# A two-layer decoder on one core: last cross-attention and feed-forward of four sequences as one unrolled block, and a new key order in the first self-attention

## The chip, the cores and the metric

The kernel runs on one core of a Trainium2 chip. Its engines are TensorE (PE, matmuls; PEld is its weight load), VectorE (DVE), ScalarE (ACT), GpSimd (POOL) and SyncE (SP, which here issues every DMA). Matmuls read SBUF and write PSUM. The metric is the device time of one execution in microseconds (us), lower is better.

## The reference, cut to what matters

The input x has 4 sequences of 1024 tokens and 256 features. Two decoder layers follow, each of self-attention, cross-attention to a context of 154 keys, and a feed-forward, each with a residual and a layer norm behind it. The change touches the first of these six parts and the last two.

```python
x = _layernorm(x + _L0_attn_ref(...))    # 16 heads of 16 features, causal bias
...
# last cross-attention: 16 heads of 16 features, padded keys masked
attn = jnp.einsum('bhqd,bhkd->bhqk', Q, K) * scale
attn = jax.nn.softmax(jnp.where(mask, -jnp.inf, attn), axis=-1)
x = _layernorm(x + out @ Wo + bo)
# last feed-forward
xr = mu_r * x + (1 - mu_r) * x_prev
xk = mu_k * x + (1 - mu_k) * x_prev
r = jax.nn.sigmoid(xr @ W_r.T)
k_act = jnp.square(jax.nn.relu(xk @ W_k.T))
x = _layernorm(x + r * (k_act @ W_v.T))
```

## The kernel before

The program has four stages, one behind the other, with a barrier of all engines between them. Stage one is the first self-attention, stage two the first cross-attention, stage three the first feed-forward with the second self-attention, and stage four the second cross-attention with the last feed-forward. Stages one to three take all four sequences in one unrolled block; stage four is a loop over the sequences (`nc.Fori(0, B)`, L1911), with a barrier at the end of each turn and semaphores that are cleared.

**Attention in two passes.** Stages one and four find the row maxima first: a first pass of scores (`first_scores` L375, `first_scores1` L2069) goes into PSUM tile psA, VectorE takes the negated maximum (L674, L2367), and the maxima are transposed, split into three bf16 parts and carried through DRAM into extra rows of the query stack (`max_dram`, `max1_dram`). A second pass (L389, L2077) has keys on the partitions and goes into psB; ScalarE takes the exponential from there into `pbuf` or `pb1` (L507, L2193), and the products with the values (`values` L400, `values1` L2091) add up in psO. Queries and keys are held as stacked bf16 parts, which also travel through DRAM. A column of ones beside the values gives the denominators; these go through DRAM to a tile of reciprocals (`reciprocals`), by which GpSimd scales the outputs (`scale_values`). psA and psB have two buffers each.

**Stage one.** The work is 128 steps, one for each of 16 head groups (4 heads of one sequence) and 8 tiles of 128 tokens. Step k issues the first pass for query tile 7 - k % 8 of group k // 8, and, 10 steps behind (LEAD), the second pass for key tile (k - 10) % 8. The mask is causal, so query tile j has j + 1 blocks of 128 keys, and key tile i has 8 - i blocks of queries. A step first issues all scores of both passes in turn, then the value products of the key tile of the step before, then a projection for another sequence if one is due (`qk_unit`, `v_unit`, `out_unit`).

**Stage four.** One turn of the loop loads the sequence, projects the keys and values of its context, transposes x, projects the queries, splits them into parts (ACT L2179 and L2182, POOL L2262, DVE L2292 and L2293), stores and loads the stack, runs the two passes over the 4 head groups with the second pass 2 groups behind (LEAD1), projects the output (L2023 and L2033), normalises, transposes, mixes each token with the one before it (ACT L2205, DVE L2390), and runs the three feed-forward products (`gemm`, L2000), with Relu and Square for the keys (L2210, L2213), Sigmoid for the gate (L2217) and the gated product on VectorE (L2396, L2399). SP stores the output tile by tile.

## Time and profile before

| what | value |
|---|---|
| three runs, median | 2812.36 us (2809.44 to 2812.92) |
| profiled execution | 2812.02 us |
| its span, first to last instruction | 2810.2 us |
| mean granted TensorE clock | 0.891 of full |
| TensorE busy in the span | 2175.3 us, 77% |
| VectorE, ScalarE, GpSimd busy | 1471.6, 1200.9, 612.2 us |

Instructions outside the span take 1.8 us of the profiled execution. In the trace, stage one lies from 0 to 914 us, stage two to 1505, stage three to 2109.8, and stage four to the end; its four turns begin near 2117, 2290, 2464 and 2637 us. A group of instructions is named by line, engine, operation and tiles; the arrow stands between what is written and what is read. All matmuls of `gemm` have one line, so those are told apart by their tiles. "Busy" of an engine is the union of its instructions' times.

### The profile page before, as it was taken

To read this page: it belongs to the slowest core of one execution; us is meant where nothing else is said; L and a number is where in the kernel's file an instruction comes from. 1 tells how busy PE (TensorE), PEld (TensorE's weight loads), DVE (VectorE), ACT (ScalarE), POOL (GpSimd) and SP (SyncE) were. 2 spreads that over 40 slices of the span, in tenths; PEclk is the share of its full clock that TensorE was granted. 3 is DMA by queue.
4 is the path that set the end of the run, shared out by engine and by line. 5 is a ranking of instruction groups with operands and counts; after the bars stand their busy time and mean duration, and the time that the engine had idled before them with its cause. 6 is when DMAs were issued, how large, how long until landed. Compare 5 with 4: busy or idle time off the path is not lost. (4 is left out here: it accounts for less than half of the span.)

```text
span 2810.2 us, 32610 instructions
## 1 busy us (share of the span) xinstructions
PE 2175.3 (77%) x11571; PEld 1209.3 (43%) x11586; DVE 1471.6 (52%) x2718; ACT 1200.9 (43%) x2635; POOL 612.2 (22%) x725
## 2 busy tenths in 40 slices
PE   4688888888887899999995348889994856747566
PEld 2233343343343555656553225556662332423324
DVE  3554465465662466666673676583543334443444
ACT  1245435435443565555552637574221332314232
POOL 4611210310011100000002665462311110211102
PEclk7899999999998899999997569999996886868768
DMA  7424324324221100000002001000007124161341
GB/s 159 112 49 90 68 59 88 70 59 70 46 65 33 50 5 18 16 18 16 8 9 68 15 0 36 6 25 12 25 17 124 36 58 64 32 103 35 69 61 31
DMA packets 129404, 135.42 MB, mean 48 GB/s; under 512 B 35405, under 2 KB 110033, under 8 KB 129170
## 3 DMA queue, kind: packets, MB, share of 16 engines
q1 hardware_dynamic: 129266, 133.62, 21.6%
q8 instruction: 82, 1.34, 0.2%
q14 instruction: 56, 0.46, 0.1%
HBM read 95.10 MB, written 38.47 MB: 48 GB/s over the span
## 5 line engine op out<-in xcount | busy, mean ns | idle before, releaser
L507 ACT ACTIVATE pbuf_sb<-psB 128x512 f32<-128x512 f32 (+1 forms) x608 | 326.7, 573 | 348.7 <-PE psB L397 342.8
L674 DVE TENSOR_REDUCE negm_sb<-psA 128x1 f32<-128x1024 f32 (+6 forms) x352 | 340.1, 1019 | 151.0 <-PE psA L385 149.7
L394 PE MATMUL psB<-qst_sb,kst_sb 99*128 99x512 bf16 (+3 forms) x768 | 234.0, 338 | 58.3 <-ACT pbuf_sb L507 47.6
L1030 ACT ACTIVATE pw_sb<-psA,nmx_sb 128x154 f32<-128x154 f32 x512 | 192.0, 387 | 194.5 <-DVE nmx_sb L1121 194.5
L383 PE MATMUL psA<-kst_sb,qst_sb 96*128 96x512 bf16 (+3 forms) x768 | 197.8, 334 | 59.9 <-DVE negm_sb L674 52.8
L1121 DVE TENSOR_REDUCE nmx_sb<-psA 128x4 f32<-128x616 f32 x128 | 102.2, 799 | 176.8 <-PE psA L898 176.8
L2193 ACT ACTIVATE pb_sb<-psB 128x512 f32<-128x512 f32 x160 | 89.0, 596 | 170.3 <-PE psB L2082 168.4
L2073 PE MATMUL psA<-kst_sb,qst_sb 97*128 97x160 bf16 x512 | 86.1, 323 | 95.8 <-issue 66.6
L411 PE MATMUL psO<-pbuf_sb,V_sb 128*32 128x512 f32 (+3 forms) x1536 | 153.6, 503 | 0.2 <-ACT pbuf_sb L507 0.2
L394 PEld LDWEIGHTS psB<-qst_sb,kst_sb 99*128 99x128 bf16 x768 | 75.1, 98 | 168.3 <-ACT pbuf_sb L507 145.5
L2367 DVE TENSOR_REDUCE negm_sb<-psA 128x4 f32<-128x640 f32 x128 | 100.0, 821 | 81.2 <-PE psA L2073 76.8
L383 PEld LDWEIGHTS psA<-kst_sb,qst_sb 96*128 96x128 bf16 x768 | 58.1, 98 | 166.2 <-DVE negm_sb L674 106.5
L1358 PE MATMUL psO<-va_sb,pat_sb 128*128 128x256 f32 x512 | 118.2, 384 | 9.8 <-DVE pat_sb L1743 9.8
L851 PE MATMUL psO<-XT_sb,wq_x_sb 128*128 128x512 f32 x256 | 122.2, 601 | 0.0
L1070 POOL TENSOR_SCALAR std_sb<-mv_sb 128x1 f32<-128x1 f32 x32 | 7.3, 228 | 503.4 <-DVE mv_sb L1148 503.4
L851 PE MATMUL psO<-wo_x_sb,ox_sb 128*128 128x256 f32 x512 | 115.4, 379 | 0.8 <-ACT ox_sb L1013 0.8
L1358 PE MATMUL psA<-qa_sb,ka_sb 128*128 128x512 f32 x256 | 115.1, 592 | 0.0
L1358 PEld LDWEIGHTS psO<-va_sb,pat_sb 128*128 128x128 f32 x512 | 97.6, 192 | 33.6 <-DVE pat_sb L1743 13.7
L2073 PEld LDWEIGHTS psA<-kst_sb,qst_sb 97*128 97x128 bf16 x512 | 52.2, 129 | 136.6 <-issue 77.3
L385 PE MATMUL psA<-masku_sb,identb_sb 128*128 128x128 bf16 x512 | 107.0, 223 | 0.0
L1716 DVE TENSOR_REDUCE nma_sb<-psA 128x1 f32<-128x1024 f32 x32 | 39.1, 1222 | 129.2 <-PE psA L1358 129.2
L1030 ACT ACTIVATION_READ_ACCUMULATOR pw_sb<-psA,nmx_sb 128x1 f32 x512 | 103.9, 203 | 0.0
(264 smaller groups left out, 4463.0 us busy)
## 6 DMA issues: line engine op xcount, KB each, us to landing
rden_sb<-dens_dram SPq DMA_DIRECT2D x128, 128.0 KB, 2.7
parts_dram<-parts_sb SPq DMA_DIRECT2D x32, 384.0 KB, 2.4
qst_sb<-parts_dram SPq DMA_DIRECT2D x96, 128.0 KB, 4.4
kst_sb<-parts_dram SPq DMA_DIRECT2D x96, 128.0 KB, 7.0
qst_sb<-parts_dram SPq DMA_DIRECT2D x48, 256.0 KB, 9.1
x_dram<-X_sb SPq DMA_DIRECT2D x64, 128.0 KB, 1.7
parts_dram<-partsb_sb SPq DMA_DIRECT2D x16, 384.0 KB, 6.9
xT_sb<-xT SPq DMA_DIRECT2D x4, 1024.0 KB, 5.1
```

Of the source, the lines that this page charges most:

```text
L383: nc.tensor.matmul(psA[:, k, at + lo:at + hi], qst[0:QK_ROWS, gg % 3, h, j * P:(j + 1) * P], kst[0:QK_ROWS, gg % 3, h, lo:hi], start=True, ...
L385: last = nc.tensor.matmul(psA[:, k, at + w - P:at + w], identb[:, :], masku[:, :], start=False, stop=True)
L394: last = nc.tensor.matmul(psB[:, k, at:at + hi - lo], kst[0:MAX_ROWS, gg % 3, h, i * P:(i + 1) * P], qst[0:MAX_ROWS, gg % 3, h, lo:hi], st ...
L411: last = nc.tensor.matmul(psO[32 * h:32 * h + 32, c, lo - c * 512:hi - c * 512], V[:, b % 2, i, at:at + 32], pbuf[:, i % 2, h, lo:hi], sta ...
L507: nc.scalar.activation(pbuf[:, i % 2, heads[0]:heads[-1] + 1, lo:hi], psB[:, (nb.n - 1) % 2, 0:len(heads) * (hi - lo)] .rearrange("p (h n) ...
L674: nc.vector.tensor_reduce(out=negm[:, gg % 2, heads[0]:heads[-1] + 1, j], in_=psA[:, (na.n - 1) % 2, :].rearrange("p (h n) -> p h n", h=le ...
L851: last = nc.tensor.matmul(dst, lhsT(i), rhs(i), start=(i == 0), stop=(i == n - 1))
L1030: last = nc.scalar.activation(pw[:, m % 2, h, :], psA[:, m % 2, at:at + K], ACT.Exp, bias=nmx[:, m % 2, h:h + 1], accum_out=psx[:, m % 3, ...
L1121: nc.vector.tensor_reduce(out=nmx[:, m % 2, :].rearrange("p (b a) -> p a b", a=2), in_=psA[:, m % 2, :].rearrange("p (a n) -> p a n", a=2) ...
L1358: last = nc.tensor.matmul(dst, lhsT(i), rhs(i), start=(i == 0), stop=(i == n - 1))
L2073: last = nc.tensor.matmul(psA[:, k, at:at + KP], qst1[0:R1, 4 * g + h, j * P:(j + 1) * P], kst1[0:R1, 4 * g + h, :], start=True, stop=True)
L2367: nc.vector.tensor_reduce(out=negm1[:, g, :, j].rearrange("p (a b) -> p a b", a=2), in_=psA[:, (na.n - 1) % 2, :].rearrange("p (a n) -> p ...
```

## The change

**Stage one.** A table KEY_ORDER gives both the key tile of the second pass and the query tile of the first pass in a step, so that every step has nine score blocks for each head. `values` is cut into the two halves of the query tokens (c = 0 and c = 1), and these are issued behind the second and behind the first unit of scores of a step.

**Stage four.** The loop is gone. One block of 24 units takes all sequences: unit gg issues the first pass of head group gg and the second pass of group gg - 2; a unit has 8 steps j. In each step, `side_tasks(gg, j)` names what else is due there: for the next sequence the transposes ("xp"), query gemms ("q"), and keys and values of the context ("kp", "vp"); for the sequence just finished its output projection ("o"); for the one before it the transposes ("xf"), the key products ("kg") and the gate and value products ("rv"). The first pass has one PSUM buffer of 1024 columns, psA[:, 0]; the side tasks share the two halves of psA[:, 1]. The query split is wholly on GpSimd, and so is the addition of the output bias. Tiles are doubled for two sequences in flight (XE, v1, v1r, kst1), the query stack has four slots and OT1 six. The barriers and clears of the loop are gone; one clear of semaphores is added behind stage one.

```diff
+    KEY_ORDER = (3, 2, 1, 0, 7, 6, 5, 4)
+    def query_tile(k):
+        return KEY_ORDER[(k - LEAD) % 8]
...
-                first = first_units(7 - k % 8) if k < UNITS else []
-                second = second_units(s % 8) if 0 <= s < UNITS else []
+                first = first_units(query_tile(k)) if k < UNITS else []
+                second = second_units(KEY_ORDER[s % 8]) if 0 <= s < UNITS else []
                 for u in range(max(len(first), len(second))):
...
+                    if u == 0 and s >= 1:
+                        values((s - 1) // 8, KEY_ORDER[(s - 1) % 8], exps_at[s - 1], 1)
+                    if u == 1 and s >= 1:
+                        values((s - 1) // 8, KEY_ORDER[(s - 1) % 8], exps_at[s - 1], 0)
...
-                if 1 <= s:
-                    values((s - 1) // 8, (s - 1) % 8, exps_at[s - 1])
...
+    nc.sync.sem_clear(range(a_full.num, x_stored.num + 1))
...
-    with top, nc.Fori(0, B) as b:
...
+        q, u = gg // 4, gg % 4
+        e, o, p = q - 2, q - 1, q + 1
+        if 0 <= e < B:
+            if u == 0 and j in (1, 3):
+                out += [("xf", e, j - 1), ("xf", e, j)]
+            if u == 0 and j in (6, 7):
+                out += [("kg", e, j - 6, 0)]
+            if u == 1 and j in (0, 1):
+                out += [("kg", e, j, 1)]
+            if u in (1, 2) and 3 <= j < 7:
+                out += [("rv", e, 4 * (u - 1) + j - 3)]
+        if 0 <= o < B and u == 3:
+            out += [("o", o, j)]
+        if p < B:
+            if u == 0 and j in (0, 2):
+                out += [("xp", p, j), ("xp", p, j + 1)]
+            if u == 0 and j in (4, 5):
+                out += [("q", p, 0, j - 4)]
+            if u == 1 and j == 2:
+                out += [("q", p, 1, 0)]
+            if u == 2 and j < 3:
+                out += [(("q", p, 1, 1), ("kp", p), ("vp", p))[j]]
...
+                for j in range(NT):
+                    if gg < GROUPS:
+                        first_scores(gg, j)
+                    if 0 <= gs < GROUPS:
+                        second_scores(gs, j // 4, j % 4)
+                        if j % 4 == 3:
+                            second_scores(gs, j // 4, 4)
+                    if j == 1 and 1 <= gs <= GROUPS:
+                        values(2 * gs - 1)
+                    if j == 5 and 0 <= gs < GROUPS:
+                        values(2 * gs)
+                    for key in side_tasks(gg, j):
...
```

On the other engines of stage four, ScalarE takes in step j its exponentials, then the copy-out in steps 2 and 6, then its part of the side task. VectorE takes the residual or gated product of the side task of step j - 1, then the maxima of step j, then the normalisation for step j - 2; the mixing is in steps 5 and 6 of a unit with u = 0, the reciprocals of group gg - 3 in step 5. GpSimd scales group gg - 3 in step 7 and adds the bias in step 5 where u = 2. SP issues in each unit the stack of the next group, then the denominators' journey of group gg - 3, then stores of parts and outputs, and the maxima last.

How the order moves, in three places.

TensorE, stage one, the end of a step with query tile 2 and key tile 3 and the value products of key tile 2, before (L383 is the first pass, L394 the second, L385 the mask, L411 the value products):

```order
L383 MATMUL psA<-kst_sb,qst_sb 128x384
L385 MATMUL psA<-masku_sb,identb_sb 128x128
L383 MATMUL psA<-kst_sb,qst_sb 128x384
L385 MATMUL psA<-masku_sb,identb_sb 128x128
L394 MATMUL psB<-qst_sb,kst_sb 128x512 x4
L411 MATMUL psO<-pbuf_sb,V_sb 32x256 x4
L411 MATMUL psO<-pbuf_sb,V_sb 32x512 x4
```

And in the change, the middle and end of the step with query tile 2 and key tile 2 (L380, L391, L382 with L394 as masks, and L408 for the value products of key tile 3; L349 is a projection):

```order
L408 MATMUL psO<-pbuf_sb,V_sb 32x512 x4
L380 MATMUL psA<-kst_sb,qst_sb 128x384
L382 MATMUL psA<-masku_sb,identb_sb 128x128
L380 MATMUL psA<-kst_sb,qst_sb 128x384
L382 MATMUL psA<-masku_sb,identb_sb 128x128
L391 MATMUL psB<-qst_sb,kst_sb 128x256
L394 MATMUL psB<-maskl_sb,identb_sb 128x128
L391 MATMUL psB<-qst_sb,kst_sb 128x256
L394 MATMUL psB<-maskl_sb,identb_sb 128x128
L408 MATMUL psO<-pbuf_sb,V_sb 32x128 x4
L391 MATMUL psB<-qst_sb,kst_sb 128x512 x4
L349 MATMUL psA<-wqkv_sb,xT_sb 128x256 x2
```

The value products stood behind all scores of a step; now one half stands behind the first unit of scores and the other behind the second, and four second-pass units follow them.

ScalarE, stage four, before (end of the feed-forward of a turn; L2217 is the Sigmoid):

```order
L2210 ACTIVATE dk_sb<-psB 128x512
L2213 ACTIVATE kact_sb<-dk_sb 128x512
L2210 ACTIVATE dk_sb<-psB 128x512
L2213 ACTIVATE kact_sb<-dk_sb 128x512
L2217 ACT_TABLE_LOAD
L2217 ACTIVATE rg_sb<-psA 128x256 x8
```

And in the change, from unit 9 on (L2338 is the Sigmoid, L2308 the exponential, L2284 and L2289 the queries):

```order
L2308 ACTIVATE pb_sb<-psB 128x512 x2
L2338 ACT_TABLE_LOAD
L2338 ACTIVATE rg_sb<-psA 128x256
L2308 ACT_TABLE_LOAD
L2308 ACTIVATE pb_sb<-psB 128x512
L2338 ACT_TABLE_LOAD
L2338 ACTIVATE rg_sb<-psA 128x256
L2308 ACT_TABLE_LOAD
L2308 ACTIVATE pb_sb<-psB 128x512
```

One load of a function table stood ahead of eight Sigmoids; now one stands ahead of each Sigmoid and one ahead of the exponential behind it. From here to the end of the block ScalarE has 41 such loads, where the loop had two in each of its four turns.

TensorE, stage four, before (feed-forward):

```order
L2012 MATMUL psB<-ident_sb,X_sb 128x128 x12
L2000 MATMUL psB<-xk_sb,wk_f_sb 128x512 x8
L2000 MATMUL psA<-wr_f_sb,xr_sb 128x256 x2
L2000 MATMUL psA<-wv_f_sb,kact_sb 128x256 x2
L2000 MATMUL psA<-wr_f_sb,xr_sb 128x256 x2
L2000 MATMUL psA<-wv_f_sb,kact_sb 128x256 x2
```

And in the change, in unit 9 (L2153 first pass, L2163 second pass, L2178 and L2182 value products, L2105 `gemm`):

```order
L2105 MATMUL psA<-wr_f_sb,xr_sb 128x256 x2
L2105 MATMUL psA<-wv_f_sb,kact_sb 128x256 x2
L2153 MATMUL psA<-kst_sb,qst_sb 128x160 x4
L2163 MATMUL psB<-qst_sb,kst_sb 128x512
L2105 MATMUL psA<-wr_f_sb,xr_sb 128x256 x2
L2105 MATMUL psA<-wv_f_sb,kact_sb 128x256 x2
L2153 MATMUL psA<-kst_sb,qst_sb 128x160 x4
L2163 MATMUL psB<-qst_sb,kst_sb 128x512
L2178 MATMUL psO<-pb_sb,v1r_sb 128x512
L2182 MATMUL psO<-pb_sb,v_sb 32x512 x4
L2105 MATMUL psA<-wr_f_sb,xr_sb 128x256 x2
L2105 MATMUL psA<-wv_f_sb,kact_sb 128x256 x2
```

The gate and value products of one sequence, two instructions each, stand now between the score passes of another.

## Rows read from the trace of the kernel before

**Rows 1.** Page, parts 1 and 2: busy shares; tenths in 40 slices of 70 us
```profile
PE 2175.3 (77%) x11571; PEld 1209.3 (43%) x11586; DVE 1471.6 (52%) x2718; ACT 1200.9 (43%) x2635; POOL 612.2 (22%) x725
...
PE   4688888888887899999995348889994856747566
...
PEclk7899999999998899999997569999996886868768
```

**Rows 2.** Busy time of each engine in stretches (from:to, length, then the columns)
```profile
core 0: us, PE busy (x) PEld busy (x) DVE busy (x) ACT busy (x) POOL busy (x), PEclk, DMA share, GB/s
124.00:844.00 720.00, 614.48 (x4125) 276.22 (x4125) 386.59 (x537) 342.04 (x630) 109.98 (x122) 0.98 0.32 66
2109.80:2157.80 48.00, 14.42 (x48) 8.99 (x48) 11.14 (x23) 9.29 (x15) 8.75 (x17) 0.68 0.72 139
2637.00:2810.20 173.20, 110.71 (x484) 60.21 (x484) 71.62 (x152) 51.14 (x88) 26.74 (x48) 0.77 0.31 59
2637.00:2693.80 56.80, 25.65 (x112) 15.49 (x112) 23.60 (x39) 8.68 (x15) 7.22 (x13) 0.65 0.73 118
2693.80:2740.00 46.20, 37.76 (x192) 13.20 (x192) 17.37 (x34) 24.34 (x45) 2.35 (x1) 0.80 0.12 29
2740.00:2757.00 17.00, 15.04 (x73) 10.04 (x73) 1.93 (x3) 2.19 (x4) 4.70 (x2) 1.00 0.23 67
2770.00:2810.20 40.20, 24.25 (x80) 16.17 (x80) 18.61 (x44) 14.13 (x22) 6.23 (x16) 0.80 0.08 26
```

**Rows 3.** Chain that ended last, in the last sequence: start us, us, what
```profile
2680.45 13.32 DMA qst_sb<-parts_dram
...
2777.90 10.18 PE psB L2000 x16
```

**Rows 4.** Stage one, 124 to 844 us: PE groups by shape; then one wait
```profile
L394 PE MATMUL psB<-qst_sb,kst_sb 99*128 99x512 bf16 x358 | 136.9, 394 | 45.2 <-ACT pbuf_sb L507 37.6
L383 PE MATMUL psA<-kst_sb,qst_sb 96*128 96x512 bf16 x346 | 121.1, 385 | 37.8 <-DVE negm_sb L674 32.0 <-DVE X_sb L628 2.2
...
ACT pbuf_sb L507 <- PE psB L397: 325.0, 204, 7.5
```

**Rows 5.** One step of stage one in time order: start us, us, what
```profile
225.96 0.60 ACT L507 ACTIVATE pbuf_sb<-psB 128x512 f32<-128x512 f32 x1 [3.27 <-PE psB L397]
...
228.85 1.71 PE L411 MATMUL psO<-pbuf_sb,V_sb 128*32 128x384 f32 x16
```

**Rows 6.** Stage four, last sequence, by shape: count | busy us, mean ns | idle before
```profile
L2023 PE MATMUL psA<-wo_x_sb,OT_sb 128*128 128x256 f32 x48 | 10.6, 381 | 0.0
L2096 PE MATMUL psO<-pb_sb,v1r_sb 128*128 128x512 f32 x16 | 9.8, 699 | 0.0
L2099 PE MATMUL psO<-pb_sb,v_sb 128*32 128x512 f32 x64 | 8.5, 605 | 0.0
L2367 DVE TENSOR_REDUCE negm_sb<-psA 128x4 f32<-128x640 f32 x32 | 25.0, 821 | 20.4 <-PE psA L2073 19.3
L2193 ACT ACTIVATE pb_sb<-psB 128x512 f32<-128x512 f32 x40 | 22.3, 596 | 42.7 <-PE psB L2082 42.2 <-PE psB L2086 0.2
L2205 ACT ACTIVATE xk_sb<-XT_sb,mu_sb 128x1024 f32<-128x1024 f32 x2 | 2.2, 1140 | 0.0
L2217 ACT ACTIVATE rg_sb<-psA 128x256 f32<-128x256 f32 x8 | 3.1, 384 | 10.2 <-PE psA L2000 10.2
L2241 POOL TENSOR_TENSOR OT_sb<-OT_sb,rden_sb 128x1024 f32<-128x1024 f32 x3 | 7.0, 2350 | 78.7 <-DMA rden_sb<-dens_dram 78.7
```

**Rows 7.** ScalarE in time order in stage three: start us, us, what
```profile
1719.64 1.06 ACT L1528 ACTIVATE cv_sb<-Y_sb 128x1024 f32<-128x1024 f32 x1
1720.72 1.28 ACT L1534 ACT_TABLE_LOAD   x1
1722.01 1.11 ACT L1534 ACTIVATE pa_sb<-psA,nma_sb 128x1024 f32<-128x1024 f32 x1
```

**Rows 8.** A hand-off in the last turn, in time order: start us, us, what
```profile
2704.98 1.09 ACT L2193 ACTIVATE pb_sb<-psB 128x512 f32<-128x512 f32 x2 [0.21 <-PE psB L2082]
...
2705.63 0.62 PE L2086 MATMUL psB<-qst_sb,kst_sb 100*32 100x512 bf16 x4 [0.20 <-ACT pb_sb L2193]
```

1184 lines of the change are left out of this document (662 added, 522 removed).

## The prediction

> **What bounds the kernel now.** I read the page first, then the busy time of stretches, then the chain, then groups of instructions. The page shows TensorE busy for 77% of the span and no other engine above 52%; the slices show where the rest is lost. TensorE stands at nine tenths in stage two and at four to seven tenths in the last ten slices, which are stage four [rows 1]. So there are two places to look at.
>
> Stage four takes 700.4 us (2109.8 to 2810.2), a lead-in of 7 us and four turns of 173.2. In the last turn no engine fills the time: TensorE is busy for 110.7 us at a mean granted clock of 0.77, VectorE 71.6, ScalarE 51.1, GpSimd 26.7 [rows 2]. The four sum to 260 us, so on average 1.5 engines work at once. The turn has a stretch of 56.8 us in which queries and keys are made and carried through DRAM (TensorE busy 25.7), 46.2 us of attention, 17.0 us until the last outputs are scaled, and what is left, 53.2 us, is projection, norm and feed-forward [rows 2]. The chain goes through a DMA of 13.3 us and a run of key products of 10.2 us with nothing beside it [rows 3]. What bounds stage four is one sequence's chain, and there are four of them in a row.
>
> Stage one is different: in 720 us TensorE is busy for 614.5 at a clock of 0.98 [rows 2], so 105.5 us are idle, most of it ahead of second-pass scores (45.2 us, waiting for ScalarE's exponentials) and ahead of first-pass scores (37.8 us, waiting for VectorE's maxima) [rows 4]. Meanwhile ScalarE waits 325 us for scores [rows 4]: each waits for the other in turn. Within a step ScalarE stands 3.27 us while TensorE does the value products, 1.71 us of them in one run, and a projection [rows 5].
>
> **Stage four, part by part.** The arithmetic is the same; what moves is when. I take the work of one sequence and spread it over four units of eight steps.
>
> TensorE: 110.7 us at clock 0.77 is 85 at the full clock, 21.3 for each unit. By kind: an f32 instruction of 256 columns is 0.22 us (10.6/48, in a stretch at clock 1.00) [rows 2, 6], so an output tile or a gate-and-value tile (8 of them), or a query or key gemm (twice the columns, 4 instructions), is 1.76 us. The value products of one half are (9.8 + 8.5)/8 = 2.3 us in a turn at clock 0.77 [rows 6]; I take 2.1, and 0.5 for the scores of one step, an estimate from their columns at the same rate.
> VectorE: 71.6 less some 11 us that go to ScalarE and GpSimd (query and key splits, bias, last scaling) is 60.5, 15 for each unit; the maxima are 0.82 a step [rows 6].
> ScalarE: exponentials 0.60 each, ten in a unit, two copies of 0.60 [rows 6]. New are table loads: 41 in place of 8, at 1.28 us each [rows 7]. That is 42 us more on ScalarE, and 40 of the 41 stand around 20 Sigmoids between exponentials.
>
> Now the length of a full unit, step by step, the longest engine in each:
> - Gate units (u = 1, 2): four steps with a Sigmoid take 0.60 + 1.28 + 0.38 + 1.28 = 3.55 us of ScalarE [rows 6, 7], with a fifth exponential or a copy in two of them 15.4 in all. The other four are TensorE's, 9.1. Together 24.5. Where u = 2, GpSimd also adds the bias (twice the elements of a scaling of 2.35 us [rows 6], so 4.7) ahead of a norm that VectorE waits for: 2 us more.
> - Output unit (u = 3): TensorE 8 x (1.76 + 0.5) + 2 x 2.1 = 22.3, VectorE nearly as much, since residual, statistics and norm join the maxima. I take 24.
> - Mixing unit (u = 0): ScalarE 4 x 1.14 for the mixing [rows 6], eight copies, two queries, two key products: 23.4 with TensorE's steps.
>
> So 24.6 for a full unit. Where tasks are missing it is less. One psA buffer for the first pass makes maxima and scores take turns, 0.5 + 0.82 and a hand-off, 1.45 us a step, 11.6 a unit: the floor. Sums: units 0 to 3, 52; 4 to 7 (no feed-forward yet, the first output unit at the end), 71; 8 to 11, 98; 12 to 15, 90; 16 and 17, 42. That is 353.
> Before unit 0: the first turn starts its scores 48 us after stage four begins [rows 2]. The query splits are now all on GpSimd, with DMAs behind them, but one barrier is gone: 45.
> After unit 17: the last denominators' journey, 17 as now (2740 to 2757) [rows 2] and 1 more; eight output tiles, which have no part done ahead any more, 14 at the full clock and 20 at a mixed one; then the rest as now, 40.2 from the last norm on [rows 2] and 3 for one buffer less: 81.
> Hand-offs: of 144 steps each has a release that its busy times don't cover; ahead of ScalarE and TensorE such gaps are 0.2 us in this trace [rows 8], and often hidden. At 0.15 a step, 21. Units 0 to 6 keep TensorE busy for half to two thirds of the time, so I add 8 for a clock of 1.2 GHz there, as now in the first stretch of a turn (0.65 [rows 2]).
> Stage four: 45 + 353 + 81 + 21 + 8 = 508 against 700.4, **192 us less**. The bounds: with no hand-offs, clock cost or port waits 479, with hand-offs three times as long 550.
>
> **Stage one.** What goes: value products no longer stand alone behind the scores. Half the products run while ScalarE and VectorE drain the first unit, half behind the second. The new order also pairs a long maximum step with a short exponential step: by blocks, VectorE's and ScalarE's work in a step now sum to nine in each, and TensorE's scores, which went from 4 to 14 blocks a step, are always nine. A step in the middle of stage one is 720/118 = 6.1 us, with TensorE busy 5.2. Taking the longest engine of each step, as above, I get 5.1 us with everything overlapped; I keep seven tenths of the difference, since part of a step stays serial, and subtract a new wait: the first value products of a group now come behind its second step's first scores, and wait for a copy-out of 0.6 us, 16 times, 10 us. That gives (6.1 - 5.1) x 118 x 0.7 - 10 = 73 us. Ends: none of it, and 105, the idle time of TensorE [rows 2]. The stall of VectorE and TensorE at each transpose of the maxima stays. The added clear of semaphores I put at 1 us or less.
>
> **The sum.** The profiled execution is 2812.0 us (its span 2810.2 and 1.8 around it), which is 0.3 below the median. 2812 - 192 - 73 = **2547 us**. Stages two and three (1196 us) keep their instructions; I put no change on them.
>
> **The rivals.**
> 1. *ScalarE's table switches cost double.* Each switch would hold ScalarE for a second 1.28 us; the gate units are its own, and 40 switches lie in five of them (9, 10, 13, 14, 17) and the next: 40 x 1.28 = 51, total 2598. Against it: in stage three an ACTIVATE ends, the load starts 0.02 us later and the next ACTIVATE starts 1.29 us after that [rows 7]. The Trainium skill, "ScalarE: Activation LUTs", section What ACT_TABLE_LOAD costs, gives 1283 ns for the load and about 1380 ns of drain, some 2.66 us for a switch. By that rule, an estimate, the 41 switches would be 109 us of ScalarE in place of 53; the trace agrees with the load and shows no drain. Chance 0.05.
> 2. *Hand-offs decide.* In-order engines with one bank for the first pass and two half banks for all side tasks: a late Sigmoid holds the gated product, which stands ahead of the maxima on VectorE, which hold the next scores. If a step costs 0.65 us rather than 0.15, 72 us come on top: 2619. For it: the many waits that are inferred between the same three engines now. Chance 0.15.
> 3. *Stage one gives nothing.* Its steps are still a run of four heavy for VectorE, then four heavy for ScalarE, and the buffers hold only two units: 2620. Chance 0.13.
> 4. *Better overlap.* Stage one gives all 105, stage four has no hand-off cost: about 2490. Chance 0.06.
> 5. *Slower: the ring closes.* If every step runs first scores, maxima, second scores, exponential, side gemm and its copy one behind the other (0.5 + 0.8 + 0.6 + 0.6 + 1.8 + 1.3 = 5.6 us), 144 steps take 806, and stage four 45 + 806 + 81 = 932, or 232 more than now: with stage one's gain, 2971. It decides from (700 - 126)/144 = 4.0 us a step on; I forecast 2.65, and the double buffers of psB and of the side tasks speak against it. Chance 0.03.
>
> **How the numbers follow.** 2547 has 0.58. The range must take in rivals 1 to 3 and stop short of 2 and 3 together (2692) and of the best ends: 2475 to 2640. About 0.2% is what a measurement of this kernel can tell from no change. Faster takes all but rival 5: 0.96; slower 0.03; 0.01 for the same.
>
> **What would show it.** Stage four near 508 us, its units 8 to 15 at 23 to 26 us each and TensorE above 80% busy there at the full clock; 41 loads of 1.28 us, with ScalarE the longest in gate units; VectorE waiting for ScalarE's gates; stage one with its second-pass wait below 25 us and a length near 840 rather than 914. Wrong would be: loads with idle time behind them (1), units of 28 us and more with no engine above 75% (2), stage one's idle time moved from scores to value products (3).

## The result, and the profile after

The changed kernel takes **2648.41 us**, median of 4 runs (2640.93 to 2653.63), against 2810.9 (2804.32 to 2812.92): ratio 0.9409, 95% interval 0.939 to 0.9429. It is 162 us faster by the medians and 166 by the ratio; the forecast said 2547, with a range that ended at 2640. The direction was right, and so was the mechanism in stage four; stage one's was not. The gain was three fifths of what I promised.

The page of the changed kernel, parts 1 and 2, answers to [rows 1]:

```profile
PE 2120.5 (80%) x11571; PEld 1193.6 (45%) x11586; DVE 1460.5 (55%) x2643; ACT 1243.4 (47%) x2672; POOL 674.2 (25%) x750
...
PE   3688888888888689999999533989899756787786
...
PEclk7799999999999899999999756999999967898898
```

The last eight slices now hold five to eight tenths where they held four to seven, and the clock is up with them.

Busy time by stretch, the columns of [rows 2]. First stage one from 124 us to its last exponential, then stage four: lead-in, units 0 to 3, 4 to 7, 8 to 11, 12 to 15, units 16 and 17, and the rest; last unit 9 alone. A unit ends at its transpose of the maxima (L2211).

```profile
core 0: us, PE busy (x) PEld busy (x) DVE busy (x) ACT busy (x) POOL busy (x), PEclk, DMA share, GB/s
124.00:869.00 745.00, 642.37 (x4365) 282.29 (x4363) 399.95 (x546) 369.78 (x679) 113.76 (x125) 0.98 0.31 65
...
2092.80:2138.80 46.00, 14.95 (x49) 8.88 (x50) 1.63 (x7) 8.51 (x15) 17.96 (x28) 0.66 0.68 168
2138.80:2207.10 68.30, 45.22 (x242) 24.88 (x242) 31.83 (x50) 20.84 (x37) 14.13 (x17) 0.77 0.46 86
2207.10:2305.30 98.20, 71.94 (x392) 39.92 (x389) 43.73 (x84) 35.47 (x65) 33.97 (x35) 0.83 0.53 113
2305.30:2421.10 115.80, 95.55 (x486) 57.04 (x484) 69.94 (x133) 68.74 (x103) 44.95 (x55) 0.90 0.39 84
2421.10:2527.40 106.30, 81.65 (x438) 47.14 (x437) 64.19 (x129) 60.61 (x88) 27.31 (x38) 0.90 0.34 76
2527.40:2567.00 39.60, 29.84 (x138) 14.39 (x136) 15.74 (x32) 34.40 (x51) 8.95 (x13) 0.97 0.18 48
2567.00:2646.00 79.00, 53.99 (x202) 38.42 (x202) 42.83 (x102) 18.89 (x32) 25.45 (x45) 0.82 0.12 39
...
2334.40:2365.00 30.60, 23.48 (x114) 12.47 (x114) 16.06 (x32) 22.46 (x31) 10.99 (x14) 0.91 0.37 82
```

The first row of stage four above begins where stage three's last work ends. From the first instruction of stage four to the end of the span it was 2109.7 to 2810.2 and is 2095.0 to 2646.0: 700.5 us became 551.0. So **149 us come from stage four and 15 from what lies ahead of it**, which is stage one (forecast 192 and 73): its last exponential ends at 869.0 where it ended at 884.1, and stages two and three gave nothing, as forecast. In stage four TensorE's idle time fell from 259.8 to 157.9 us and its busy time from 440.7 to 393.1, at a mean clock of 0.77 and now 0.85.

What TensorE waits for in stage four, and under it VectorE (engine, tile, line, releaser: us in all, times, longest):

```profile
PE psA L2153 <- DVE negm_sb L2481: 48.8, 43, 4.9
PE psA L2153 <- DMA kst_sb<-mask_dram: 20.0, 3, 9.5
...
PE psA L2211 <- DVE negm_sb L2481: 14.5, 11, 3.1
...
DVE rg_sb L2527 <- ACT rg_sb L2338: 53.8, 21, 12.9
```

The second row is a wait that I had not foreseen: units 4, 8 and 12 begin a sequence and find its keys not there. The third row is the transpose at a unit's end. And stage one, TensorE by line, 124 to 844 us, two lines of before and then the changed kernel:

```profile
L394 PE MATMUL psB<-qst_sb,kst_sb 99*128 99x512 bf16 (+2 forms) x706 | 213.6, 335 | 51.8 <-ACT pbuf_sb L507 43.8
L383 PE MATMUL psA<-kst_sb,qst_sb 96*128 96x512 bf16 (+3 forms) x697 | 177.6, 330 | 50.6 <-DVE negm_sb L674 44.3 <-DVE X_sb L628 2.2 <-DVE V_sb L620 0.2
```

```profile
L391 PE MATMUL psB<-qst_sb,kst_sb 99*128 99x512 bf16 (+2 forms) x734 | 221.5, 332 | 39.5 <-ACT pbuf_sb L512 31.7
L380 PE MATMUL psA<-kst_sb,qst_sb 96*128 96x512 bf16 (+3 forms) x703 | 178.7, 332 | 22.0 <-DVE negm_sb L679 20.0
L408 PE MATMUL psO<-pbuf_sb,V_sb 128*32 128x512 f32 (+3 forms) x1456 | 157.8, 506 | 7.4 <-ACT OT_sb L498 7.4
...
L454 PE MATMUL psA<-ident_sb,negm_sb 128*32 128x128 f32 x15 | 4.6, 307 | 20.8 <-DVE negm_sb L679 20.8
```

The idle time ahead of first-pass scores has shrunk from 50.6 to 22.0 us, and 20.8 us stand where none stood before: the transpose of a group's maxima, 1.4 us each time. With 5.3 us ahead of two projections, what TensorE waits for VectorE is nearly what it was, and its idle time in these 720 us is 98.0 against 105.5. In the new order the first pass of a group ends on query tile 6 (four maxima of 896 columns), where it ended on tile 0.

### The profile page after: what moved, and what is told of

Read it like the earlier page. It is cut to its first block and busy times, and to the rows that moved or that the text cites. A ratio compares the mean times of both kernels' runs of the same rounds, so it can differ in the third digit from the quotient of the medians.

```text
span 2646.0 us, 32547 instructions
## 1 busy us (share of the span) xinstructions
PE 2120.5 (80%) x11571; PEld 1193.6 (45%) x11586; DVE 1460.5 (55%) x2643; ACT 1243.4 (47%) x2672; POOL 674.2 (25%) x750
## 5 line engine op out<-in xcount | busy, mean ns | idle before, releaser
L679 DVE TENSOR_REDUCE negm_sb<-psA 128x1 f32<-128x768 f32 (+6 forms) x352 | 346.9, 1022 | 159.1 <-PE psA L382 156.6
L391 PE MATMUL psB<-qst_sb,kst_sb 99*128 99x512 bf16 (+3 forms) x768 | 232.3, 332 | 42.9 <-ACT pbuf_sb L512 34.7
L380 PE MATMUL psA<-kst_sb,qst_sb 96*128 96x512 bf16 (+3 forms) x768 | 198.2, 337 | 28.5 <-DVE negm_sb L679 25.4
L408 PE MATMUL psO<-pbuf_sb,V_sb 128*32 128x512 f32 (+3 forms) x1536 | 168.0, 510 | 8.7 <-ACT OT_sb L498 7.4
L2308 ACT ACTIVATE pb_sb<-psB 128x512 f32<-128x512 f32 x160 | 92.2, 598 | 150.3 <-PE psB L2163 149.9
L391 PEld LDWEIGHTS psB<-qst_sb,kst_sb 99*128 99x128 bf16 x768 | 74.3, 98 | 179.7 <-ACT pbuf_sb L512 146.3
L2153 PE MATMUL psA<-kst_sb,qst_sb 97*128 97x160 bf16 x512 | 64.4, 255 | 88.1 <-DVE negm_sb L2481 48.8
L380 PEld LDWEIGHTS psA<-kst_sb,qst_sb 96*128 96x128 bf16 x768 | 60.3, 99 | 153.0 <-DVE negm_sb L679 93.6
L551 POOL TENSOR_TENSOR OT_sb<-OT_sb,rden_sb 128x1024 f32<-128x1024 f32 x15 | 35.4, 2360 | 289.8 <-DMA rden_sb<-dens_dram 289.8
L382 PE MATMUL psA<-masku_sb,identb_sb 128*128 128x128 bf16 x512 | 107.2, 224 | 0.0
```

The costliest lines, as they stand in the source:

```text
L380: nc.tensor.matmul(psA[:, k, at + lo:at + hi], qst[0:QK_ROWS, gg % 3, h, j * P:(j + 1) * P], kst[0:QK_ROWS, gg % 3, h, lo:hi], start=True, ...
L382: last = nc.tensor.matmul(psA[:, k, at + w - P:at + w], identb[:, :], masku[:, :], start=False, stop=True)
L391: last = nc.tensor.matmul(psB[:, k, at:at + hi - lo], kst[0:MAX_ROWS, gg % 3, h, i * P:(i + 1) * P], qst[0:MAX_ROWS, gg % 3, h, lo:hi], st ...
L408: last = nc.tensor.matmul(psO[32 * h:32 * h + 32, c, lo - c * 512:hi - c * 512], V[:, b % 2, i, at:at + 32], pbuf[:, i % 2, h, lo:hi], sta ...
L679: nc.vector.tensor_reduce(out=negm[:, gg % 2, heads[0]:heads[-1] + 1, j], in_=psA[:, (na.n - 1) % 2, :].rearrange("p (h n) -> p h n", h=le ...
L2308: nc.scalar.activation(pb1[:, v % 2, h, :], psB[:, (nb.n - 1) % 2, :], ACT.Exp).then_inc(b_free, 1)
```

## The experiments

Fifteen kernels, in five parts. Each is the changed kernel with an edit; medians are of 4 runs, the ratio is to the kernel before on the same chip. The changed kernel's ratio is 0.9409, and its interval is 0.2% to either side, so I call two of them different from about 8 us on. Microseconds worked out from ratios use 2811.

Each kernel also left one trace, and a trace tells the stages apart. Two lengths serve below. From 124 us to stage one's last exponential: the five kernels with the change's stage one (the changed kernel, s4_keys_early, s4_gate_copy, s4_exp_gate, s4_half_banks) take 741.9 to 749.5 us, mean 745.2. From stage four's first instruction to the end: the eight kernels with the change's stage four take 545.0 to 554.5 us, the changed kernel 551.0. What lies outside such a spread is hardly chance.

### Which half of stage one's change gained

**s1_old**: key order 0 to 7, first pass 7 to 0, value products behind the step's scores.

> The changed kernel with stage one as it was before (keys 0 to 7 in order, value products of both halves behind the step's scores); stage four as changed. Prices stage one's part of the change by itself. By the trace (in the changed kernel stage four begins 14.7 us earlier) it should take 2663 us, 15 more than the changed kernel. The 73 us of my prediction would make it 2721. If stage four's form is slowed or sped by anything that stage one leaves behind, the difference is neither.

Measured 2664.32 us (2660.58 to 2666.48), 0.9471 (0.9453 to 0.9489).

**s1_order_only** (new order, old places) and **s1_place_only** (old order, new places):

```diff
-                    if u == 0 and s >= 1:
-                        values(..., exps_at[s - 1], 1)
-                    if u == 1 and s >= 1:
-                        values(..., exps_at[s - 1], 0)
...
                 if qk_unit(k):
                     project_qk(*qk_unit(k))
+                if s >= 1:
+                    for c in (1, 0):
+                        values(..., exps_at[s - 1], c)
```
```diff
-    KEY_ORDER = (3, 2, 1, 0, 7, 6, 5, 4)
+    KEY_ORDER = (0, 1, 2, 3, 4, 5, 6, 7)
...
-        return KEY_ORDER[(k - LEAD) % 8]
+        return 7 - k % 8
```

> The changed kernel with stage one's nine-block key order kept, and the value products put back behind the step's scores and projections, both halves together. With the run that has neither (2664 us) and the changed kernel (2648) it splits stage one's 16 us. Theory P (the place of the value products is what gained; the order only evens blocks that nobody waited for): 2660 to 2668. Theory O (the order gained): 2645 to 2652. Theory X (each cost something that the other hides: the order gives runs of four steps heavy for one engine, and a transpose of the maxima behind a heavy step): over 2668.

> The changed kernel with stage one's keys in the old order (0 to 7, queries 7 to 0), and the value products in halves between the scores, as changed. Theory P: 2645 to 2652, or less, down to 2628, since the transpose of the maxima (TensorE waits 20.8 us for it in the changed kernel, none before) then comes behind a light step again. Theory O: 2660 to 2668.

Measured: order only **2683.87** us, 0.9556 (0.9539 to 0.9573); place only **2641.3** us, 0.9409 (0.9379 to 0.9438). From 124 us to the last exponential of stage one (windows of each trace; idle is length less busy):

| | length | TensorE busy | idle | clock |
|---|---|---|---|---|
| neither (s1_old) | 761.2 | 647.4 | 113.8 | 0.97 |
| order only | 784.5 | 676.8 | 107.7 | 0.93 |
| place only | 739.3 | 636.0 | 103.3 | 0.97 |
| both (the change) | 745.0 | 642.4 | 102.6 | 0.98 |
| both, keys interleaved | 768.6 | 648.8 | 119.8 | 0.96 |

```profile
124.00:908.50 784.50, 676.80 (x4354) 295.99 (x4355) 390.34 (x544) 368.55 (x678) 112.44 (x123) 0.93 0.30 61
```

The gain is the places' (17 us by the ratios in the old order, 41 in the new). The order by itself costs 24 us. And it costs this **not in idle time** (6 us less of it) but in busy time: 29 us more for the same matmuls, at a mean clock of 0.93 and not 0.97; busy time times clock is 629 in one and 628 in the other. The clock records of the two traces say the same: TensorE is busy for 98 us at the lower of the two levels (half of full) against 44, and half of the difference is 27 us. Over the whole execution the mean clock was 0.905 or 0.906 in all four runs of order only, and 0.912 to 0.915 in all four of s1_old. Theory X is the one that fits, for a cause that it did not name.

Beside the new places the ratios of the whole kernels show no cost of the order (0.9409 in both), but the traces do. Five kernels have place only's stage one (it and the four combined ones below): 734.5 to 739.4 us to the last exponential, mean 738.0, all shorter than the shortest of the five with both (741.9, mean 745.2). So the nine-block order costs 7 us there too. The place of the value products removed 10 us of idle time in the old order and 5 in the new, and in the new order it kept the clock up.

**s1_inter**, keys 3, 6, 1, 4, 7, 2, 5, 0 (with both copy-outs after the last step):

> The changed kernel with stage one's keys in the order 3, 6, 1, 4, 7, 2, 5, 0, so that a step heavy for VectorE (key 4 and up) stands beside one heavy for ScalarE, and the first pass of a group ends on a light step (key 2) in place of key 6, ahead of the transpose of the maxima. Both halves of the value sums now end with the last step, so both copy-outs follow it. Theory A (the runs of four heavy steps, and the transpose behind a heavy one, are what kept stage one's gain small): TensorE's waits in it, 98 us in 720, fall by a third to a half, the transpose's 20.8 us most of all: 2605 to 2620 us. Theory B (each step is a chain of scores, maxima, exponentials with buffers for two units, whatever the order): within 5 us of 2648, with the transpose's wait gone to others. Theory C (the second copy-out of 0.6 us now stands in TensorE's way 16 times): up to 10 us slower, 2658.

Measured 2676.99 us (2673.62 to 2687.65), 0.9526 (0.95 to 0.9552): 33 us slower. The transpose's wait went to nothing, and the wait of first-pass scores for VectorE grew from 22.0 to 49.1 us:

```profile
L391 PE MATMUL psB<-qst_sb,kst_sb 99*128 99x512 bf16 (+3 forms) x696 | 213.9, 338 | 44.2 <-ACT pbuf_sb L512 39.3
L380 PE MATMUL psA<-kst_sb,qst_sb 96*128 96x512 bf16 (+3 forms) x694 | 180.5, 338 | 49.1 <-DVE negm_sb L679 47.9 <-DVE V_sb L625 1.0
```

All three theories fall, since none reached 2677. Interleaving the heavy steps did not help; but this kernel also has both copy-outs behind the last step, which theory C priced at up to 10 us, so how much of the loss is the order's isn't shown.

**s1_late_transpose**, the transpose behind the second unit of the next group:

```diff
+                    if u == 1 and 0 < k <= UNITS and k % 8 == 0:
+                        pe.wait_ge(a_free, na.n - (2 if k < UNITS else 0))
+                        a = slot_a()
+                        nc.tensor.transpose(...)
...
-                if k < UNITS and k % 8 == 7:
-                    pe.wait_ge(a_free, na.n)
```

> The changed kernel with its nine-block order, and stage one's transpose of a group's maxima moved from the end of the group to behind the second unit of the next group's first step, on TensorE and VectorE alike (and SyncE's journey of them one step later). Takes away the wait of 1.4 us, 20.8 us in 15 times, in which TensorE stands until VectorE is through with a heavy step. Theory W (that wait is what the new order gives back): 2626 to 2636 us, which would also make the new order no worse than the old one with the same places (2641). Theory M (VectorE's backlog stays, so the wait moves to the next first-pass scores, as it did when the keys were interleaved): 2643 to 2650. It does not tell where VectorE's backlog comes from.

Measured 2641.16 us (2637.81 to 2651.73), 0.9394 (0.9367 to 0.9421). The wait at the transpose fell from 20.8 to 2.4 us, that of first-pass scores rose from 22.0 to 32.2, and the two projections' from 5.3 to 9.6: most of the 18.4 us moved, and TensorE's idle time in 124 to 844 us went from 98.0 to 95.7 only. The time lies between the theories, and its interval meets the changed kernel's. To the last exponential this kernel takes 738.0 us, below the five with both changes and like the five of place only (734.5 to 739.4); it is one trace.

### What holds stage one

**s1_half_maxima** leaves half of the keys out of the maxima:

```diff
-        [:, :, 0:(j + 1) * P], axis=AX_X, op=ALU.max,
+        [:, :, 0:(j + 1) * P // 2], axis=AX_X, op=ALU.max,
```
**s1_half_exps** does the same to the exponentials: columns `lo` to `(lo + hi) // 2` alone.

> The changed kernel; in stage one VectorE's maxima read half of their columns, so half of the keys are left out of the maxima (the first-pass scores are all made). Takes some 130 us of work from VectorE and none from the others. Theory R (VectorE and ScalarE each stand in a ring with TensorE through two buffers; TensorE's idle 102.6 us in stage one are halves of these rings): TensorE's wait ahead of first-pass scores and transposes (22.0 + 20.8 + 5) goes, 30 to 45 us less, 2603 to 2618. Theory T (TensorE's own time is the floor, 642 us of busy time in 745, and what one ring gives the other takes): under 15 us, 2633 to 2648.

> The changed kernel; in stage one ScalarE's exponentials take half of the columns, so half of each tile's exponentials are left out and the value products read a constant there (the products are all made). Takes some 130 us of work from ScalarE. Theory R: the wait ahead of second-pass scores (39.5 us) and a part of the value products' goes, 30 to 45 us less, 2603 to 2618. Theory T: under 15 us. If this is much more or less than the half maxima give, one of the two rings holds the stage by itself.

Measured: half the maxima **2590.79** us, 0.9216 (0.9196 to 0.9236); half the exponentials **2623.78** us, 0.9334 (0.9314 to 0.9354). TensorE's groups in stage one, 124 to 780 us, first with half the maxima, then with half the exponentials:

```profile
L391 PE MATMUL psB<-qst_sb,kst_sb 99*128 99x512 bf16 (+2 forms) x707 | 212.6, 330 | 37.6 <-ACT pbuf_sb L512 30.2
L380 PE MATMUL psA<-kst_sb,qst_sb 96*128 96x512 bf16 (+3 forms) x700 | 175.3, 328 | 4.8 <-DVE negm_sb L679 4.6
```
```profile
L391 PE MATMUL psB<-qst_sb,kst_sb 99*128 99x512 bf16 (+3 forms) x664 | 190.1, 335 | 19.2 <-ACT pbuf_sb L512 19.2
L380 PE MATMUL psA<-kst_sb,qst_sb 96*128 96x512 bf16 (+3 forms) x664 | 174.3, 341 | 25.5 <-DVE negm_sb L680 24.1
```

Each takes away its own wait (the exponentials half of it) and leaves the other's: two rings with TensorE, as theory R says. VectorE's is the tighter: 54 us for 132 us of its work (more than my bound of 45), 21 for 120 us of ScalarE's. To the last exponential, half the maxima take 51 us less, of which 31 are idle time of TensorE (102.6 to 71.4) and 20 its busy time (642.4 to 622.2, clock 0.98 and 0.99); why the same matmuls are busy for less isn't shown. With half the exponentials it is 17 us less, 16 of them idle time. The work of VectorE in this stage, 400 us in 745, is on the path although it is busy for half of the time.

### Stage four: the keys and the first pass

**s4_keys_early**:

```diff
+                if u == 3 and q + 1 < B:
+                    move_keys(q + 1)
                 if 0 <= gg - 3 < GROUPS:
                     reciprocals(gg - 3)
...
-                    if u == 3:
-                        move_keys(q + 1)
```

> The changed kernel with one move on SyncE's queue in stage four: the next sequence's keys (store, six loads, mask) are sent at the beginning of the unit before the sequence's first, ahead of the journey of the denominators, not behind it. Theory A (TensorE's waits for the keys at units 4, 8 and 12, 9.5 + 5.4 + 5.0 = 20.0 us in the trace, are a late send, and nothing else is late then): 2628 to 2632 us. Theory B (the maxima or the stacks are just as late, or the denominators now hold the output projection instead, whose first product already waits 1.2 to 4.5 us): 2640 to 2650.

Measured 2634.2 us (2629.47 to 2639.75), 0.9362 (0.9339 to 0.9386): 13 to 14 us. Stage four takes 538.0 us in its trace, 7 below the shortest of the eight that have the change's. The 20 us of waits for keys are gone, those for maxima grew from 48.8 to 60.4 us, and unit 3 from 18.5 to 24.8: theory A, with a part of theory B.

**s4_half_banks**: scores, semaphore and maximum in two halves of two heads (VectorE's part of the edit):

```diff
-                dve.wait_ge(f_full, nf.up())
-                nc.vector.tensor_reduce(out=negm1[:, gg % 2, :, j]...
+                for a in range(2):
+                    dve.wait_ge(f_full, nf.up())
+                    nc.vector.tensor_reduce(out=negm1[:, gg % 2, 2 * a:2 * a + 2, j], ...
```

> The changed kernel with stage four's first pass in two halves of two heads, each with its own bank, semaphore count and maximum: scores of one half while VectorE reads the other. 128 maxima of 640 columns (0.82 us) become 256 of 320. Theory A (one buffer for the first pass is what makes TensorE wait, 48.8 us for VectorE in stage four and most of VectorE's 126.7 us for scores): 15 to 35 us less, 2613 to 2633. Theory B (VectorE is late because of what stands ahead of the maxima, Sigmoid's gates and statistics, and with twice the instructions it is no earlier): 2640 to 2655.

Measured 2638.7 us (2632.11 to 2643.62), 0.9394 (0.9379 to 0.941): 4 us by the ratio and 10 by the medians. By the times this is not told apart from the changed kernel. In its trace stage four takes 540.7 us, 4 below the shortest of the eight, and TensorE's wait for maxima went from 48.8 to 31.5 us. Neither theory's number; the single buffer is probably a cost, a smaller one than its row.

### Stage four: the 40 table loads

One gate step of unit 9, from the timeline of the changed kernel (start us, us, engine and line, [idle before it]):

```profile
2353.06 1.28 ACT L2338 ACT_TABLE_LOAD   x1
...
2353.57 0.45 PE L2153 MATMUL psA<-kst_sb,qst_sb 97*128 97x160 bf16 x4 [1.51 <-DVE negm_sb L2481]
...
2354.36 0.38 ACT L2338 ACTIVATE rg_sb<-psA 128x256 f32<-128x256 f32 x1
2354.76 1.28 ACT L2308 ACT_TABLE_LOAD   x1
2354.84 0.42 DVE L2527 TENSOR_TENSOR rg_sb<-psA,rg_sb 128x256 f32<-128x256 f32 x1 [1.33 <-ACT rg_sb L2338]
...
2356.02 1.13 PE L2105 MATMUL psA<-wr_f_sb,xr_sb 128*128 128x256 f32 x4
2356.05 0.60 ACT L2308 ACTIVATE pb_sb<-psB 128x512 f32<-128x512 f32 x1
2356.32 0.80 DVE L2481 TENSOR_REDUCE negm_sb<-psA 128x4 f32<-128x640 f32 x1
2356.66 1.28 ACT L2338 ACT_TABLE_LOAD   x1
2356.99 1.03 PE L2105 MATMUL psA<-wv_f_sb,kact_sb 128*128 128x256 f32 x4
```

ScalarE goes load, Sigmoid, load, exponential and load again with no gap, 3.60 us a step (3.55 forecast). Of the 41 loads 35 have their ACTIVATE 0.03 us behind them or less, four have 0.10 us, waiting for a gate product, and two 0.95, waiting for second scores. Rival 1 is refuted. By the Trainium skill, "ScalarE: Activation LUTs", section What ACT_TABLE_LOAD costs, a drain of about 1380 ns would follow; here a load starts at 2354.76, takes 1.28, and the exponential begins at 2356.05. VectorE has its maxima behind the gated product, which waits 1.33 us for the Sigmoid. So are these loads what holds a gate unit?

**s4_gate_copy** leaves the Sigmoid out:

```diff
-    ... ACT.Sigmoid).then_inc(gate_made, 1)
+    ... ACT.Copy).then_inc(gate_made, 1)
```

> The changed kernel with Copy in place of Sigmoid in the gate of the last feed-forward: the Sigmoid is left out, and nothing else; the 40 table loads around it fall away. Theory A (the loads lie in the ring of the gate units: TensorE's scores, ScalarE's Sigmoid and loads, VectorE's gated product and the maxima behind it): units 9, 10, 13 and 14 (30.6, 28.9, 25.9, 27.0 us) lose 4 to 8 us each, 2618 to 2632 in all. Theory B (ScalarE has time for them, as its 150 us of waiting for scores say; the ring is TensorE's and VectorE's): 2640 to 2648.

Measured 2638.17 us (2636.06 to 2640.18), 0.9389 (0.9373 to 0.9405): 53 us fewer of ScalarE (all 41 loads are gone) gave 6 us by the ratio, which is not told from nothing, and 10 by the medians. The trace gives more: stage four takes 534.8 us, 16 less than the changed kernel and 10 less than the shortest of the eight, while this kernel's stage one happened to take 4.5 us longer, with the same instructions. Units 9 and 10 went from 30.6 and 28.9 to 28.7 and 27.3, and what lies behind unit 15, where ScalarE was busiest (87% in units 16 and 17), from 118.6 to 109.9. So the loads are worth some 6 to 16 us, about half of it at the end, and inside the full units theory B holds, nearly: in a gate step TensorE does 1.13 + 1.03 + 0.45 + 0.38 us for gate, value, first and second scores (L2163, 0.38), and every fourth step 2.1 us of value products: 3.5 a step, almost as much as ScalarE.

**s4_exp_gate**:

```diff
-    ... ACT.Sigmoid).then_inc(gate_made, 1)
+    ... ACT.Exp, scale=-1.0).then_inc(gate_made, 1)
...
+                link(nc.vector.tensor_scalar(rg[:, at % 2, :], rg[:, at % 2, :], 1.0, None, ALU.add))
+                link(nc.vector.reciprocal(rg[:, at % 2, :], rg[:, at % 2, :]))
```

> The changed kernel with the gate of the last feed-forward computed as 1 / (1 + exp(-x)): ScalarE does Exp in place of Sigmoid, so its 41 table loads of 1.28 us shrink to one or two, and VectorE gets two more instructions of 256 columns for each of 32 gates (about 0.6 us together). Theory A (in the gate units the ring goes through ScalarE: VectorE waits 53.8 us in stage four for Sigmoids, in front of the maxima): units 9, 10, 13, 14 go from 30.6, 28.9, 25.9 and 27.0 us to 23 to 25, and the time to 2620 to 2632. Theory B (hand-offs and VectorE's own order hold the ring, the loads lie in ScalarE's waiting time, of which it has 150 us for scores): 2644 to 2660, since VectorE works 20 us more.

Measured 2684.53 us (2680.32 to 2687.59), 0.954 (0.9519 to 0.9561): 37 us slower. My price for the addition was wrong. VectorE by shape in 2340 to 2375 us of this kernel:

```profile
L2528 DVE RECIPROCAL rg_sb<-rg_sb 128x256 f32<-128x256 f32 x4 | 7.0, 1753 | 0.1
...
L2527 DVE TENSOR_SCALAR rg_sb<-rg_sb 128x256 f32<-128x256 f32 x4 | 1.2, 289 | 3.9 <-ACT rg_sb L2338 3.9
```

Two instructions are 2.04 us, not 0.6: 65 us more on VectorE for 32 gates. Since the loads were worth 6 to 16 by themselves, those 65 us cost some 43 to 53. That points at VectorE as the engine with the least room in the gate units. It doesn't prove it: adding work to one engine and taking it from another are different tests, the two instructions stand in line between Sigmoid and gated product, and TensorE's clock fell too (2334.4 to 2393.8 us: 0.83, against 0.91 in the changed kernel). No run takes work from VectorE there.

### Putting the gains together

**combined**: s1_place_only, s4_keys_early, s4_half_banks, and stage four's transposes behind the next unit's first scores. **combined_recip_late** and **combined_gate_after** change VectorE's order in it, **combined_keys_earlier** SyncE's, on top of the last:

```diff
-                    if j == 5 and 0 <= gg - 3 < GROUPS:
+                    if j == (5 if u == 2 or gg >= GROUPS else 7) and 0 <= gg - 3 < GROUPS:
                         reciprocals(gg - 3)
```
```diff
-                    if key and key[0] == "rv":
-                        gated(*key[1:])
                     if gg < GROUPS:
                         maxima(gg, j)
+                    if key and key[0] == "rv":
+                        gated(*key[1:])
```
```diff
-                if u == 3 and q + 1 < B:
-                    move_keys(q + 1)
...
+                if u == 2 and q + 1 < B:
+                    move_keys(q + 1)
                 if gg < GROUPS:
                     move_maxima(gg)
```

> Everything that gained by itself, together: stage one's keys in the old order with the value products at their new places; stage four's keys sent early; its first pass in two half banks; and stage four's transposes of the maxima behind the next unit's first scores, where TensorE waited 14.5 us for VectorE. If the gains add up: 7 (place only against the changed kernel) + 14 (keys) + 10 (half banks) + 5 to 14 (transposes), 2603 to 2612 us. If the waits they remove are the same ones, or VectorE's and ScalarE's own work is by now the bound of stage four: 2615 to 2628.

> The combined kernel with VectorE's reciprocals of the denominators two steps later in three units of four (all but the unit before the output projection), so that VectorE does not wait for their DMA (8.8 to 14 us in stage four) with the maxima behind it. Theory A (in-order VectorE passes this wait on to TensorE's scores; with the keys sent first, unit 3 had grown from 18.5 to 24.8 us by it): 5 to 10 us below the combined kernel. Theory B (the journey comes late anyhow and now holds GpSimd and the output projection): the same or up to 5 us slower.

> The combined kernel with VectorE's gated product behind the maxima of the same step, not ahead of them. Theory A (a Sigmoid with its loads holds the gated product, which holds the maxima, which hold TensorE's next scores, 8 steps a sequence): 4 to 12 us below the combined kernel. Theory B (in these steps ScalarE, 3.6 us with two loads, is the longest engine, and TensorE almost as long; who stands first on VectorE changes nothing, and the side tile comes free later): within 3 us, or up to 8 us slower.

> The combined kernel with the gated products behind the maxima (2617.7 us), and SyncE sending the next sequence's keys another unit earlier, ahead of the maxima's journey in unit 2 of a sequence, so that the denominators' journey of unit 3 does not start behind them. There VectorE waited 15.5 us for the denominators and TensorE 14.1 for VectorE in the first sequence. Theory A (SyncE's order made that wait): unit 3 falls from 26.2 us to 17 or 18, and the time to 2600 to 2608. Theory B (the denominators' DMAs are slow there by themselves, beside stacks and stores of queries): 2614 to 2620.

| | median us (runs) | ratio, 95% interval |
|---|---|---|
| combined | 2619.8 (2619.21 to 2633.98) | 0.9325 (0.9296 to 0.9355) |
| combined_recip_late | 2642.51 (2636.12 to 2650.74) | 0.9388 (0.936 to 0.9416) |
| combined_gate_after | 2617.69 (2615.66 to 2619.88) | 0.9299 (0.9283 to 0.9315) |
| **combined_keys_earlier** | **2607.6** (2606.11 to 2608.44) | **0.9279** (0.9259 to 0.9299) |

The gains did not add up. In the combined kernel one wait for VectorE is 14.0 us long, in unit 3 (26.1 us): SyncE sends the keys first and the denominators behind them, and VectorE's reciprocal waits for these (15.4 us the longest, 8.3 with the keys earlier still) with the maxima behind it. TensorE's longest wait for maxima in 2138 to 2240 us, combined and combined_keys_earlier:

```profile
PE psA L2154 <- DVE negm_sb L2485: 24.3, 14, 14.0
```
```profile
PE psA L2154 <- DVE negm_sb L2485: 18.1, 14, 6.9
```

With the keys another unit earlier, unit 3 falls from 26.2 us (combined_gate_after) to 19.0, stage four from 530.5 to 520.3, and the whole by 6 us by the ratios, whose intervals meet, and 10 by the medians: SyncE's order made that wait, though not all of it, since 6.9 us remain. The reciprocals two steps later cost 18 us: VectorE's norms now wait 23.0 and 22.4 us for GpSimd's inverse deviations (L2538, L2517), which stand behind the later scaling, where the combined kernel has 8.2 and 1.7; and the 9.7 us wait for keys at one unit is back. The gated product behind the maxima is worth 7 us by the ratio, 2 by the medians and nothing in stage four's length (530.7 and 530.5), so it is not told from nothing. The best kernel here is 1.4% below the changed one (0.9279/0.9409).

## Why the prediction was right and wrong

**What bounds the kernel.** The time came out 101 us over the forecast, 58 of them in stage one (73 forecast, 15 measured) and 43 in stage four (508 and 551). Right for stage four, as the traces read: one sequence's chain four times in a row was the cost, and overlapping the four gave 149 us, 102 of them TensorE's idle time. No run takes this part of the change apart, so what the missing barriers, the doubled tiles and the moved query split give by themselves is not shown. Wrong for stage one: I took 105 us of idle time as something that an interleaved order removes. (A slip of reading in it: of the last ten slices of [rows 1] one stands at eight tenths, not all at four to seven.)

**Stage four's terms.** Lead-in: 45 forecast, 43.8 measured (2095.0 to 2138.8). After unit 17: 81, and 79.0. TensorE's work: 85 us a sequence at the full clock, 340 in all; busy time times clock summed over the seven stretches above is 337 (an estimate, since the clock is a mean over the stretch). The loads: 41 of 1.28 us, as forecast. The failing step of stage four is the units with their two additions, 353 + 21 + 8 = 382 us, measured 2138.8 to 2567.0, **428**, which is 2.97 us a step and not 2.65:

| units | forecast, and hand-offs | measured | TensorE idle | clock |
|---|---|---|---|---|
| 0 to 3 | 52 + 5 | 68.3 | 23.1 | 0.77 |
| 4 to 7 | 71 + 5 | 98.2 | 26.3 | 0.83 |
| 8 to 11 | 98 + 5 | 115.8 | 20.2 | 0.90 |
| 12 to 15 | 90 + 5 | 106.3 | 24.6 | 0.90 |
| 16 and 17 | 42 + 2 | 39.6 | 9.8 | 0.97 |

The largest miss is in units 4 to 7, 22 us, and not where the loads are. By stretches, TensorE's busy time less its product with the clock is 10 + 12 + 10 + 8 + 1 = 41 us (by the trace's clock records it is busy for 71 us at the lower level, which makes 36), for which I had taken **8 for the clock**, in units 0 to 6 alone: it stayed at 0.90 through the full units, at which I had it at 1. The idle time is 428 less 324 busy, 104 us, against 382 less 283 less 8, some 91, in my sum. So the clock was mis-sized by 28 to 33 us, the idle time by 13. This is a sum of TensorE's time, not an experiment: no run holds the clock up and leaves the rest, so that the 28 to 33 us would come back isn't shown. (Unit 13 ran at 1.00 and took 26.0 us; its neighbour 14, at 0.87, took 27.0.) I had summed the longest engine of each step as if the next step's engine never waited, and 0.15 us a step for the rest. Of the idle time the runs name 13 us for the keys, 4 to 10 for the single buffer; 6 to 16 us of the whole go with the loads.

Unit lengths show the same: 8 to 11 took 29.1, 30.6, 28.9 and 27.2 us where I had 23.4, 24.5, 26.5 and 24, with TensorE at 77, 77, 82 and 95% and a clock near 0.9 (forecast: above 80% at the full clock).

**A wait that I left out.** The change put the keys' send behind the denominators' journey on SyncE, 20.0 us of TensorE's time. I had gone through TensorE, ScalarE and VectorE step by step and not through SyncE's queue.

**Stage one.** 73 forecast, 15 came. The term that failed is (6.1 - 5.1) x 118 x 0.7: the mean step, from exponential to exponential over 112 steps, went from 6.10 to 5.96 us, and with half of the maxima's columns it is still 5.54. The estimate of 5.1 took VectorE and ScalarE as working beside each other through whole steps; with two buffers each they did not, and the runs with half the maxima and half the exponentials show that TensorE waits on both. The 5.1 could have been refused beforehand: it lies below TensorE's own busy time of 5.2 us a step, so (6.1 - 5.1) x 118 is 118 us out of 105 that were idle, and seven tenths of it asks for most of them. The copy-out's 10 us were 7.4. "The stall of VectorE and TensorE at each transpose of the maxima stays" was wrong: for TensorE there was none, and the new order made one, of 20.8 us, of which most moves on when it is taken away. And the nine-block order was no gain: 24 us slower alone, 7 beside the new places.

**The rivals.** 1 (doubled table switches) refuted. 3 (stage one gives nothing) came true but for 15 us. Of its two reasons, the buffers that hold only two units fit the runs with half the work; the runs of four heavy steps do not, as far as s1_inter shows it, since breaking them up made it worse. 2 (hand-offs) named 72 us and the units took 46 more than the sum, but only 13 of them are idle time of TensorE; most of the rest is clock, which no rival had. 4 and 5 did not come. The range went wrong in one place, where it was to "stop short of 2 and 3 together": they had 0.15 and 0.13, but both rest on the same optimism, engines that overlap up to the longest, and misses of both kinds came together, 43 and 58 us.

## What to carry to other kernels

An estimate by "the longest engine of each step" is a floor, not a forecast: with two buffers between three in-order engines, halve or double one engine's work in mind and ask who waits; here a third of VectorE's time in stage one was worth 54 us. And hold the estimate against each engine's own busy time a step: it can't be less. When a loop is unrolled into one stream, walk the DMA queue's order too: every wait on it delays all that is sent behind. Price TensorE at the clock that comparable stretches of the trace show, and not at the full clock: the attention of the last turn [rows 2] had TensorE busy for 82% at a clock of 0.80, and the full units, at 77 to 95%, then had 0.90.

## What the runs showed of the hardware

- The granted clock can fall without long waits. TensorE's waits in 124 to 844 us, order only:

```profile
PE psB L391 <- ACT pbuf_sb L507: 38.8, 128, 0.5
PE psA L380 <- DVE negm_sb L674: 28.8, 56, 2.2
PE psA L449 <- DVE negm_sb L674: 14.4, 14, 1.0
```

  The longest is 2.2 us, and the mean clock 0.94 there (0.93 over the whole stage); the kernel with neither change has waits up to 4.6 us and 0.97 in the same window. The Trainium skill, "TensorE: Matmul & The Clock Gate", section A second HAM failure mode: psum-queue depth-cycling, tells of short idle times between groups of matmuls that make the clock swing; the trace fits (from 124 us to the last exponential 25 stretches at the lower level, 102 us in all, against 8 and 47 us in the kernel with neither change), and no run here isolates it.
- VectorE's reciprocal of 256 columns takes 1753 ns where the TENSOR_SCALAR of the same size that adds 1 takes 289 (s4_exp_gate).
- Table loads take 1.28 us each, and 35 of 41 have their ACTIVATE 0.03 us behind them or less, with no drain between; the other six wait for TensorE.
- Traces of the same instructions in stage one differ by up to 8 us in 745 (five kernels, 741.9 to 749.5).
